# A four-layer cross-attention kernel on one core: head weighing in pairs of pairs and a moved output product in the two wide layers, and a feed-forward whose second product is made from rounded halves

## The reference, cut to what matters

```python
# layer 0
x = residual + softmax(Q K^T / sqrt(16)) V @ wo + bo
y = layer_norm(x) @ w1 + b1          # 256 -> 1024
y = gelu(y) @ w2 + b2                # 1024 -> 256
x = x + y
# layer 1 (wide): q = rms_norm(x) @ wq, k = ctx @ wk, v = ctx @ wv, heads of 64
x = x + softmax(q k^T) v @ wo
# layer 2 (wide): as layer 1 with rope(q), rope(k), a mask on the keys,
# and at its end x = layer_norm(x + out)
# layer 3 (narrow, 16 heads of 16)
x = x + softmax(Q K^T / sqrt(16)) V @ Wo + bo
```

## Time and profile before

| | |
|---|---|
| runs | median 2268.0 us of 3 (2266.34 to 2273.81) |
| the profiled execution | 2268.11 us, of which the profiler's span is 2266.2 us |
| PE matmul busy | 2062.2 us, 91% |
| DVE busy | 1425.7 us, 63% |
| ACT busy | 1263.5 us, 56% |
| POOL busy | 581.4 us, 26% |
| feed-forward | from 370.40 to 481.39 us |
| wide layers up to the first scores | 481.39 to 515.38 us |
| wide layers, samples 0 to 15 | 515.38 to 1175.26 us |
| wide layers, samples 16 to 31 | 1175.26 to about 1916 us |

### The profile page before, as it was taken

How to read it: one execution, slowest core, us unless ns; L and a number is a source line. 1 busy time by engine, 2 the same in 40 slices (tenths; PEclk the granted TensorE clock), 3 DMA queues, 4 the chain that set the end, 5 groups by cost and what they waited for, 6 DMA issues and landing times. The chain is left out here.

```text
span 2266.2 us, 50658 instructions
## 1 busy us (share of the span) xinstructions
PE 2062.2 (91%) x18696; PEld 1678.8 (74%) x18696; DVE 1425.7 (63%) x2880; ACT 1263.5 (56%) x3225; POOL 581.4 (26%) x676
## 2 busy tenths in 40 slices
PE   6888986979999999999989999899999998889897
PEld 5777775867787787787767777777777776777776
DVE  5777774335445455454587777777777775577775
ACT  3677774335555555555555555555555554577775
POOL 3232320000000000000055655655556551000000
PEclk8999997989999999999999999999999999799999
DMA  6444332011000000000001000000000000344432
GB/s 170 135 136 139 117 122 82 0 52 58 14 8 8 14 8 15 8 8 14 9 15 35 15 9 9 9 9 15 9 9 10 1 1 1 115 121 121 121 122 71
DMA packets 72965, 109.69 MB, mean 48 GB/s; under 512 B 7062, under 2 KB 62618, under 8 KB 72730
## 3 DMA queue, kind: packets, MB, share of 16 engines
q1 hardware_dynamic: 72442, 105.98, 15.4%
q10 hardware_dynamic: 288, 0.51, 0.1%
HBM read 69.28 MB, written 37.19 MB: 47 GB/s over the span
## 5 line engine op out<-in xcount | busy, mean ns | idle before, releaser
L1444 ACT ACTIVATE wide_P<-PS,MX 100x361 f32<-100x361 f32 x512 | 288.9, 564 | 415.3 <-DVE MX L1562 411.4
L1562 DVE TENSOR_REDUCE MX<-PS 100x2 f32<-100x722 f32 x256 | 231.5, 904 | 181.4 <-PE PS L1312 181.3
L626 ACT ACTIVATE L_P<-PS,MX 100x361 f32<-100x361 f32 x512 | 253.5, 567 | 132.2 <-DVE MX L752 132.2
L752 DVE TENSOR_REDUCE MX<-PS 100x2 f32<-100x722 f32 x256 | 219.9, 900 | 48.3 <-PE PS L512 47.7
L1738 POOL TENSOR_TENSOR wide_AC<-wide_T,wide_COSM 128x362 f32<-128x362 f32 x128 | 118.0, 922 | 409.4 <-DVE wide_SH L1520 408.1
L1335 PE MATMUL PS<-wide_PT,wide_V 128*64 128x100 f32 (+1 forms) x3072 | 189.1, 257 | 29.6 <-issue 29.6
L524 PE MATMUL PP<-CON,L_P 100*128 100x100 f32 x1536 | 183.9, 257 | 26.6 <-DVE L_PT L759 20.7
L1335 PEld LDWEIGHTS PS<-wide_PT,wide_V 128*64 128x64 f32 (+1 forms) x3072 | 139.4, 136 | 84.4 <-issue 68.2
L524 PEld LDWEIGHTS PP<-CON,L_P 100*128 100x128 f32 x1536 | 151.5, 144 | 47.8 <-ACT L_P L626 34.3
L1321 PE MATMUL PP<-CON,wide_P 100*128 100x100 f32 x1536 | 179.6, 254 | 0.8 <-ACT wide_PT L1451 0.5
L1321 PEld LDWEIGHTS PP<-CON,wide_P 100*128 100x128 f32 x1536 | 164.6, 144 | 10.4 <-issue 2.0
(11 more groups left out here) (255 smaller groups left out, 5434.4 us busy)
## 6 DMA issues: line engine op xcount, KB each, us to landing
strips<-L_KS SPq DMA_DIRECT2D x256, 90.5 KB
L_KA<-strips SPq DMA_DIRECT2D x64, 362.0 KB, 3.1
C<-ctx_t SPq DMA_DIRECT2D x32, 361.0 KB, 3.1
kept<-L_CTH SPq DMA_DIRECT2D x16, 361.0 KB, 4.9
kept<-L_CTL SPq DMA_DIRECT2D x16, 361.0 KB, 5.5
L_CTH<-kept SPq DMA_DIRECT2D x16, 361.0 KB, 4.3
L_CTL<-kept SPq DMA_DIRECT2D x16, 361.0 KB, 5.1
C<-in_ctx SPq DMA_DIRECT2D x16, 256.0 KB, 3.4
```

The lines of the kernel that those rows point to most:

```text
L626: nc.scalar.activation(P[:, (4 * g + j) % 8, 0:SK], PSB[0:SQ, j, 0:SK], ACT.Exp, bias=MX[:, s % 2, 4 * q + j:4 * q + j + 1], scale=1.0).th ...
L752: nc.vector.tensor_reduce(MX[:, s % 2, 4 * q + 2 * i:4 * q + 2 * i + 2], PSB[0:SQ, 2 * i:2 * i + 2, 0:SK], AX.X, ALU.max, negate=True).the ...
L1444: nc.scalar.activation(P[:, (2 * g + i) % 4, 0:SK], PS_[i][0:SQ, 0:SK], ACT.Exp, bias=MX[:, s % 2, h:h + 1], scale=1.0, accum_out=DEN[:, s ...
L1562: nc.vector.tensor_reduce(MX[:, s % 2, 2 * p:2 * p + 2], PSB[0:SQ, 0:2, 0:SK], AX.X, ALU.max, negate=True).then_inc(Z["maxed"], 1)
```

## The change

It has four parts. In the wide layers two pairs of heads are weighed together: `weigh(g-3)` and `weigh(g-2)` at the end of each odd slot and none at the end of an even one; `PT` holds six heads instead of four for that, and `after_weigh` is gone, so that scores always follow a weighing or the `after_turn` jobs. The jobs move: O from slot 3 to slot 5, V to slots 0, 2, 3, 4, 6 and 7; `post_stats` goes from slot 4 to 6 and `post` from 6 to 7. `C` has one slot in the wide layers, so that a context is loaded one sample ahead and not two, and PE waits for `WO` only at its first use. The feed-forward is written out without loops; its second product takes the rounded halves of W2 and of the hidden tile, comes out transposed, gets its bias on ACT, and is transposed back on PE (`back`) before DVE adds it.

```diff
 # wide_layers, jobs_at
-                if p == 3 and s > 0:
+                if p == 5 and s > 0:
                     after_turn.append(("O", s - 1, 0))
                 if p == 5 and s < NS:
                     after_turn.append(("R", s, 0))
-                if p in (3, 4, 5) and s < NS:
-                    after_turn.append(("V", s, 3 + p - 3))
-                if p in (5, 6, 7) and s + 1 < NS:
-                    after_weigh.append(("V", s + 1, p - 5))
+                if p in (2, 3, 4) and s < NS:
+                    after_turn.append(("V", s, 3 + p - 2))
+                if p in (6, 7) and s + 1 < NS:
+                    after_turn.append(("V", s + 1, p - 6))
+                if p == 0 and 0 < s < NS:
+                    after_turn.append(("V", s, 2))
...
                     context(0)
-                    context(1)
                     load_output_weights(sp, "L1")
...
                     for s in range(NS):
-                        if s + 2 < NS:
+                        if s + 1 < NS:
                             sp.wait_ge(Z["c_low"], KE * (s + 1))
-                            context(s + 2)
+                            context(s + 1)
...
-                    pe.wait_ge(wo_in["L1"], 16)
                     pe.wait_ge(Z["padded"], 1)
...
                         for key in after_turn:
                             job(key)
-                        if 2 <= g <= HP * NS + 1:
+                        if g % 2 and 3 <= g <= HP * NS + 1:
+                            weigh(g - 3)
                             weigh(g - 2)
-                        for key in after_weigh:
-                            job(key)
...
-                            if p == 4 and s < NS:
+                            if p == 6 and s < NS:
                                 post_stats(s - 1)
-                            if p == 6 and s < NS:
+                            if p == 7 and s < NS:
                                 post(s - 1)
 # feed_forward, PE
+                    def output(u):
+                        i, t = divmod(u, nf)
+                        pe.wait_ge(Z["w2_low"], 1)
+                        pe.wait_ge(Z["hid_low"], u + 1)
...
+                            for m, (x, y) in enumerate(((W2H, HH), (W2H, HL), (W2L, HH))):
+                                last = nc.tensor.matmul(outs[i % 2][k][:, 0:GS], x[:, t, c], y[:, u % 4, :], start=t == 0 and m == 0,
+                                                        stop=t == nf - 1 and m == 2)
...
+                    for u, i, t in stream():
+                        if u < U:
+                            hidden(u)
+                        if u >= 2:
+                            output(u - 2)
+                        if i + 1 < groups and t in (3, 4):
+                            turn(i + 1, t - 3)
+                        if 0 < i < groups and t in (5, 6):
+                            back(i - 1, t - 5)
 # feed_forward, ACT and DVE, for each hidden tile u
+                        nc.scalar.activation(H32[:, u % 3, :], hid[u % 2][:, 0:GS], ACT.Gelu, bias=col("b1", u % nf)).then_inc(Z["hid_taken"], 1)
...
+                        nc.scalar.activation(HH[:, u % 4, :], H32[:, u % 3, :], ACT.Copy).then_inc(Z["hid_high"], 1)
...
+                        nc.vector.tensor_tensor(HL[:, u % 4, :], H32[:, u % 3, :], HH[:, u % 4, :].bitcast(fp32), ALU.subtract).then_inc(Z["hid_low"], 1)
...
+                    split_w1(0)
+                    normalise(0)
+                    split_w1(1)
```

More of the change, by code:

```diff
@@ L151, in _ @@
                 eng.memset(MV[:, :, :], 1.0)
-        PASSED[:] = [sem("passed")]
-        S = {k: sem("ffn_" + k) for k in
-             ("high_w", "low_w", "product", "taken", "rounded", "split", "summed", "added", "stats", "moments", "powers", "rstd", "normed")}
         s_out = sem("out_written")
@@ L998, in _ @@
-                    gain(0, 0)
-                    def body(i, last_group):
-                        for t in range(nf):
-                            act.wait_ge(S["product"], i * per + (HID + t + 1))
-                            nc.scalar.activation(HT[:, t, :], banks[(HID + t) % nb][:, 0:G * SQ], ACT.Gelu, bias=col("b1", t)).then_inc(S["taken"], 1)
-                        if not last_group:
-                            gain(i, TURN)
-                        act.wait_ge(S["summed"], i * G + 1)
-                        for g in range(G):
-                            n = (TURN if last_group else OUT) + g
-                            act.wait_ge(S["product"], i * per + (n + 1))
-                            nc.scalar.activation(P[:, g, 0:E], banks[n % nb][0:SQ, 0:E], ACT.Copy).then_inc(S["taken"], 1)
@@ new lines, in _ @@
+                    act.wait_ge(wo_in["ffn"], 16)
+                    nc.scalar.activation(W2H[:, :, :], w2, ACT.Copy).then_inc(Z["w2_high"], 1)
+                    for u, i, t in stream():
+                        if u < U:
+                            hidden(u)
+                        if i and t == 2 and i < groups:
+                            output(i - 1)
+                        if i + 1 < groups and t in (3, 4):
+                            gain(i + 1, t - 3)
+                    output(groups - 1)
@@ L1480, in _ @@
                             unload(g - 1)
-                        for key in after_turn + after_weigh:
+                        for key in after_turn:
                             job(key)
```

327 lines of the change are left out of this document (190 added, 137 removed).

## The result

The changed kernel took 2177.5 us (median of 4 executions, 2175.2 to 2180.8) against 2270.7 us before (4 executions, 2266.3 to 2273.8): ratio 0.959, 95% interval 0.957 to 0.962, 93 us less. 2175 us was predicted. The profiled execution of the changed kernel has a span of 2178.0 us, that of before 2266.2, so 88.2 us are to be found in the two traces.

| stage | before | after | difference | predicted |
|---|---|---|---|---|
| up to the feed-forward | 370.7 | 373.1 | +2.3 | 0 |
| feed-forward | 110.7 | 91.0 | -19.7 | -19.7 |
| its end to the first scores | 34.0 | 33.2 | -0.8 | -1.5 |
| first wide layer (samples 0 to 15) | 659.9 | 638.7 | -21.2 | -21.0 |
| second wide layer, to its last scores | 737.9 | 690.1 | -47.8 | -51.1 |

What follows compares the result with a forecast made beforehand. PE was taken to bound the feed-forward and first wide layer, PE or a chain between maxima the second; -19.7 - 1.5 - 21.0 - 51.1 = -93.3 us from 2268.1 gives 2175 us, 2135 to 2205 at 8 in 10.

Steps and rivals of the forecast that it cites:

- Feed-forward, -19.7: Feed-forward stage: cheaper second product, added transposes back and an earlier first product sum to -19.7 us, between -15 and -22.
- Start of the wide layers, -1.5: Before the first scores: of 3.3 us from dropping the WO wait, about 1.5 stay, as ACT awaits sample 1's context.
- Weighing in pairs, -1.1 per sample: Wide layers: a pair's second weighing costs 0.5 us, not 0.67; with the entry, -1.1 us per sample (-0.7 to -1.7).
- The term of -0.10 us per pair for its entry: Pair weighing: the second weighing's entry from other tiles is gone, taken at -0.10 us a pair (0 to 0.25).
- First wide layer, -21.0: PE-bound layer: -1.1 us per odd sample, -1.8 per even one, 2.5 from sample 0; 21.0 us gained (14 to 28).
- Second wide layer, -51.1: Second wide layer: -7.3 us per odd and even pair, seven pairs, -51.1 us; bounds -15 and -102.
- Without O, slot 3 falls to that chain with the context's split on top, 6.3, and in the even sample to 5.2: -2.7 and -3.0: Second wide layer: moving O out shortens slot 3 from 8.99 us (odd) and 8.17 (even), by -2.7 and -3.0.
- -0.4 and -1.8: Second wide layer, slots 4 and 5 together: 10.8 us in even and 11.75 in odd samples, though O comes into slot 5.
- From slot 7 to slot 2 of the next sample I expect nothing: Second wide layer: no gain there, since DVE waits for POOL's tables and V in slots 0 and 2 fills PE's idle time.
- The half clock comes back behind another gap: Rival, chance 0.24: PE's clock falls in slot 5, lengthening a sample by about 1.7 us; 25 us, 2200 us total.
- More is won: Rival, chance 0.20: DVE starts earlier and the second wide layer becomes PE-bound; -102 us instead of -51, 2124 us.
- The feed-forward's table reload: Rival, chance 0.03: ACT reloads its table between Gelu and Copy, feed-forward does not gain; 20 to 50 us lost.

Runs made afterwards that it cites:

- the run with one weighing a slot: The changed kernel with each slot weighing its own pair of heads again, all else as in the changed kernel: 2174.1 us.
- the run with the feed-forward alone: The kernel before with the changed feed-forward and nothing else, wide layers as before: 2247.8 us.
- The filler: The changed kernel with three more matmuls (0.7 us, result overwritten) ahead of V in slot 4 of the second wide layer's odd samples: 2172.3 us.

## Why the prediction was right, and where it was not

**Feed-forward, -19.7.** Right, in the sum and in its terms: blocks 1.10 us (1.09), the second half of W1's splitting beside the normalising as described. Two terms were off in opposite directions: a set of four transposes back costs PE's stream 0.35 us from its start to the next product (0.5 predicted), so six of them 0.9 less, and the first product started 9.3 us after the stage's beginning instead of 12.8, -3.5 where -4.2 stood. That the sum fits to 0.1 us is in part luck.

**Start of the wide layers, -1.5.** Mechanism right: the wait for WO went, and ACT's wait for the context of sample 1 came, at 498.38 us. The size, -0.8, is inside the bounds, but it hangs on the clock at that place: 33.2 us there, 30.1 in the run with one weighing a slot, from code that is the same up to this point. What the stretch won in that run, sample 0 gave back (38.1 us instead of 34.3), so the two are better read together: 71.2 us before and 67.5 in the changed kernel, -3.7, where -1.5 and -2.5 stood.

**Weighing in pairs, -1.1 per sample.** Mechanism right in the first layer, size wrong: 0.60 to 0.70, less than the smallest bound (0.7). The two weighings of a pair take 1.19 us to the scores and one takes 0.67, as predicted (1.17), so a pair saves 0.15 and a sample 0.60. The term of -0.10 us per pair for its entry is what failed: nothing of it shows. The rule of the Trainium skill, TensorEngine Tiling (Array Packing), Key Properties, that a change of the tiling mode drains the engine, agrees in direction: an odd sample of the first layer lost seven such changes and 1.31 us (43.12 to 41.81), where 1.2 was worked out. But the price per change is not one figure: the four that pairing removes gave 0.60 us (0.15 each, which a cheaper second weighing explains as well), the three that came from the V behind the weighing, which V spread alone removes, 0.75 (43.12 to 42.37; 0.25 each). No run shows a drain by itself.

**First wide layer, -21.0.** The sum is right (-21.2), and so are even samples (-1.9 for -1.8) and odd ones (-1.3 for -1.1), but each is made of other parts than the text had: in even samples pairing gave 0.66 and V spread 1.27 (1.1 and 0.7 predicted), in odd ones 0.60 and 0.75 (1.1 and nothing). So the agreement to 0.2 us is luck. Sample 14 was taken at nothing and became 3.7 us longer: DVE and ACT are busy with the next layer's weights in slot 3, and PE, which used to work O there, had nothing. Sample 0 gave 3.0.

**Second wide layer, -51.1.** The sum is near (-47.8), its attribution wrong. The step that failed is "Without O, slot 3 falls to that chain with the context's split on top, 6.3, and in the even sample to 5.2: -2.7 and -3.0", together with "-0.4 and -1.8" for slots 4 and 5, into which O comes. The interval of slot 3 fell just so (4.85 and 6.32 us), but O's place accounts only for 2.4 and 0.4 us of it (7.27 and 6.68 with O in slot 3), and slot 5 pays 3.2 and 2.0 for that (4.07 and 5.40 to 7.31 and a mean of 7.39), so that the layer is 14 us longer than with O in slot 3.

What carried the gain is the V spread, which gives 58 us in this layer with O left in slot 3. At most 33 of them are the clock, which fell behind PE's idle time in slot 2 and made slot 3 long. The other 25 are PE's work taken out of slot 5, where two V stood and PE set the pace, into slots 0 and 2, where it was idle. Filling slots 0 and 2 is not the only way to keep the clock up in slot 3: moving O with the later post-norm also took the gap of 1.87 us out of slot 2, and the falls out of slot 3. And the gap alone does not decide whether the clock falls, as the run with the feed-forward alone shows.

The text's "From slot 7 to slot 2 of the next sample I expect nothing" is right for V: spread alone, it leaves slots 0 to 2 as they were. But the changed kernel takes 1.0 and 1.1 us less from slot 1 to 2 (5.30 to 4.29, 6.68 to 5.55), with 0.5 more in slot 0 of odd samples, and that comes with the later post-norm, which the text priced in slots 4, 6 and 7 alone.

Slots 4 and 5 were predicted at 10.8 and 11.75 us and took 11.2 and 13.0. The odd ones would be at 11.9 without the falls of the clock. O takes 3.45 us there, not 3.27. And PE is not "over 2 us ahead of the chain" at the end of slot 5: the earlier trace rows already show DVE waiting 2.13 and 1.36 us for PE ahead of slot 6's maximum, and in the changed kernel it waits 1.50 and 1.23. Slots 6 and 7 of odd samples cost 1.1 us more, where 0.3 stood. That all this adds up to within 3 us of the forecast is luck.

**The rivals.** "The half clock comes back behind another gap" was given 0.24 and came true in part, in the slot it named, with 1.6 us a time (1.7 predicted) in 5 of 7 odd samples. It did not decide, since the falls of before had cost more (72 us at 1.2 GHz in the wide layers, 27 after). The rule of the Trainium skill, TensorE: Matmul & The Clock Gate, "HAM oscillation", which ties the fall to long idle gaps, disagrees with the trace here too: gaps of 1.63 us inside a busy sample were enough in five samples, and were not in two with the same gap. "More is won" did not come: PE is still idle 2.6 to 3.4 us in a sample. The feed-forward's table reload did not come either.

What stays open: why the same gap is followed by a fall in one sample and not in the next (and in one execution and not in another, as the run with the feed-forward alone shows), and where a fall goes when its gap is closed. The filler shows that it can go elsewhere; no run here tells beforehand where.

## What to carry to other kernels

A job moved from a full slot into a nearly empty one can pay twice: the full slot gets shorter, and where the idle time that it fills was followed by a fall of the clock, the slot behind it does too. So look at PE's granted clock in the slot behind each gap, not only at the gap. When several parts change at once, a right total says little about the parts; the largest interval that shrinks (here slot 3 without O) need not be where the gain comes from, and undoing one part at a time found a version 17 us better than the change as a whole (2160.1 us, with O in slot 3, V in slots 0, 2, 4, 5, 6 and 7, and the context first). Work taken off an engine where another one sets the pace is worth nothing, and may open the gap that costs the clock.

## What the runs showed of the hardware that was not expected

- The clock fell to 1.2 GHz behind gaps of 1.4 to 3.5 us in a stream in which PE was some 90% busy or more, for 3.4 or 6.8 us at a time, and in the same slot sample after sample: in the kernel before at the end of slot 2 of every odd sample from 19 to 29, and in slot 3 of the even ones between them.
- What a fall costs depends on where it comes. One of 3.4 us costs 1.6 us in slot 5 of the changed kernel, where PE is the bound; the 6.8 us in slots 2 and 3 of before go with 2.9 us (11.57 against 8.70 for slot 3); in slot 1 of an even sample it cost 0.6 to 0.9 us of the sample with the filler, and nothing that shows in the interval in the kernel before with O in slot 5.
- The same kernel's executions spread by up to 1.1% (2254.1 to 2278.7 us), and mostly with their mean granted clock (0.969 in the shortest, 0.960 in the longest).
- More work made the program no slower: 0.7 us of products that nobody reads, in 8 samples, with a median of 2172.3 against 2177.5 us.
